# Macaron layer on one core: the minimum of the next unit moved ahead of P's low half on VectorE

## The chip, the cores and the metric

The kernel runs on one core of a Trainium2 chip. The metric is the device time in microseconds (us) of one execution, as the median of the runs.

## The reference

The input x is 4 x 256 tokens of width 512. Three residual steps follow one another:

```python
x = x + 0.5 * ffn(layernorm(x))      # dense 512x512 + bias + LoRA mixture, 8 experts of rank 16, top 2
x = x + attn(layernorm(x), wq, wk, wv, wo)
x = x + 0.5 * ffn(layernorm(x))
```

Attention has 32 query heads and 8 key/value heads of width 128, rotary embedding on q and k, a causal window of 128 keys, a softmax over each row, P times V, and the output projection `out @ wo`. All is float32. The kernel reaches that accuracy by splitting operands into a high and a low half (`_hi`, `_lo`) and adding three products.

## The kernel before

The middle part, some six sevenths of the time, is attention. It walks over eight **groups** g, one for each key/value head with its four query heads. Group 0 and group 7 are written out; groups 1 to 6 are a hardware loop on each engine. A group has two **halves** hf (two batches each), and a half has eight **slots** s, one for each **unit** u = 16g + 8hf + s: one batch with one query head. The order of work on each engine is written by hand, and every engine takes its own list in order; semaphores tie the lists together. Inside a slot of unit u:

- **TensorE (PE)**: at the first slot of a half (in the last half: at its third) the transposes of V (`v_transpose`, L1182), which wait for V's difference of the half before; a chunk of 9 matmuls of the projection that makes q, k and v of the next half (`project`, L1173; other counts in the first and last group); the scores of unit u+1 (`scores`, L1192 to L1195); the transposes of P of unit u-1 (`p_transpose`, L1203), which wait for the low half of P of unit u-2, since both use the one PSUM bank T; then, in slots 1 and 5, P times V (`values`, L1216), and in slots 2, 3, 6 and 7 the output projection (`out_project`, L1234).
- **VectorE (DVE)**: the softmax normalisation of unit u (`softmax_norm`, L918 and L921), which waits for the exponentials; where a projection ended in the slot before, the rotary sum (`rope_sum`, L888, both inputs in SBUF); where one ends now, the cosine product (`rope_cos`, L879); P's low half of unit u-1 (`p_lo`, L928), which waits for ScalarE's high half; in a slot where V's projection ends, V's difference (`v_diff`, L894); then the mask, fold and minimum of unit u+1 (`softmax_min`, L907 to L913), which waits for the scores of u+1; in slots 1 and 5 the low halves of the attention output (`o_lo`, L934); additions into x (`x_add`, L941) at slots 0, 3, 4 and 7.
- **ScalarE (ACT)**: exponentials of unit u (`softmax_exp`, L606), high halves of weights (L552), the rotary swap of a projection (`rope_swap`, L580), P's high half of unit u-1 (`p_hi`, L614), high halves of q and k (`rope_hi`, L588). In slots 1 and 5 `p_hi` also waits until `values` has read the old P.
- **GpSimd (POOL)**: the rotary sine product (`rope_sin`, L401), a masked copy of P (`p_part`, L408), which waits for `p_lo` of the same unit, the low half of q or k (`rope_lo`, L418), and the low halves of the weights (`split_lo`, L393): four of wo in slot 4 of a group's first half, which `out_project` needs in slot 6.

SP issues the weight loads, each when a slot of the ring of raw weights has been split.

V's projection ends in slot 7 of each half (in the last group in slot 1 of its second half), so `v_diff` runs there and `v_transpose` is the first work of TensorE in the next slot.

Of the kernel before, what the change touches and what calls it, by code (L numbers as in the profile page):

```python
# [46 lines left out]
SLOTS = 8  # L47
# [13 lines left out]
def ended(first, last, hf, s):  # L61

    if s < 0:
        return ended(first, last, 0, SLOTS - 1) if hf else None
    pos = spread(first, last, hf)
    return next((m for m in range(6) if pos[s] < 12 * (m + 1) <= pos[s + 1]), None)


def v_slot(last, hf):

    return 2 if last and hf else 0


def target(g, last, hf):

    return 2 * g + 1 if last else 2 * g + hf + 1
# [25 lines left out]
def macaron(nc, x_in, wq, wk, wv, wo, w_base, b_base, w_router, lora_a, lora_b, ident_in, mask_in, side_in, rope_in, out):  # L102
    ctx = ExitStack()
    with ctx:
# [126 lines left out]
        def wait(eng, s, n):  # L231

            if not isinstance(n, int) or n > 0:
                eng.wait_ge(s, n)
# [523 lines left out]
        def _(dve):  # L758
# [115 lines left out]
            def rope_cos(j, m):  # L874

                r = 5 * j + m
                dve.wait_ge(swap_done, r + 1)
                wait(dve, qlo_done, {0: r, 1: r - 2}.get(m, r - 1))
                nc.vector.tensor_tensor(rot[:, m % 2, :].rearrange("p (b s) -> p b s", b=2),  # L879
                                        A[m % 2][:, :].rearrange("p (b s) -> p b s", b=2),  # L880
                                        rope[:, 0 if m == 0 else 2, :].unsqueeze(1).broadcast_to([P, 2, SEQ]),
                                        ALU.mult).then_inc(a_free, 1)

            def rope_sum(j, m):
                r = 5 * j + m
                dve.wait_ge(t2_done, r + 1)
                dve.wait_ge(a_free, 6 * j + m + 1)
                nc.vector.tensor_tensor(rot[:, m % 2, :], rot[:, m % 2, :], swap[:, m % 2, :],  # L888
                                        ALU.add).then_inc(sum_done, 1)

            def v_diff(j):

                dve.wait_ge(vcopy_done, j + 1)
                nc.vector.tensor_tensor(v_half(swap[:, 1, :], 1), v_half(A[1][:, :], 1), v_half(swap[:, 1, :], 0),  # L894
                                        ALU.subtract).then_inc(vdiff_done, 1)

            def v_lo(j, par):
                dve.wait_ge(vhi_done, j + 1)
                nc.vector.tensor_tensor(v[1][:, par, :, :], A[1][:, :].rearrange("p (t n) -> p t n", t=HT),  # L899
                                        v[0][:, par, :, :].bitcast(F32), ALU.subtract).then_inc(a_free, 1)  # L900

            def softmax_min(u, s):

                dve.wait_ge(s_done, u + 1)
                wait(dve, exp_done, u - 1)
                sc = S[s % 2]
                nc.vector.tensor_tensor(sm[:, s % 2, 0:P], sc[:, P:2 * P], mask[:, 0:P], ALU.add).then_inc(part_done, 1)  # L907
                nc.vector.copy_predicated(sc[:, 2 * P:3 * P], mask[:, P:2 * P].bitcast(I32), sc[:, 3 * P:4 * P]).then_inc(part_done, 1)
                dve.wait_ge(part_done, 2 * u + 2)
                nc.vector.memset(gate[:, :], 0.0)  # L910
                nc.vector.tensor_tensor_reduce(sm[:, s % 2, 0:P], sc[:, 0:P], sm[:, s % 2, 0:P], 1.0, FMAX,
                                               ALU.add, ALU.min, nmax[:, s % 2, 0:1])
                nc.vector.tensor_reduce(nmax[:, s % 2, 1:2], sc[:, 2 * P:3 * P],  # L913
                                        axis=mybir.AxisListType.X, op=ALU.min).then_inc(min_done, 1)

            def softmax_norm(u, s):
                dve.wait_ge(exp_done, u + 1)
                nc.vector.reciprocal(rinv[:, s % 2, :], rsum[:, s % 2, :]).then_inc(rinv_done, 1)  # L918
                dve.wait_ge(rinv_done, u + 1)
                wait(dve, t_done, u - 1)  # L920
                nc.vector.tensor_tensor(prob[:, s % 2, 0:2 * P].rearrange("p (c n) -> p c n", c=2),  # L921
                                        S[s % 2][:, 0:2 * P].rearrange("p (c n) -> p c n", c=2),
                                        rinv[:, s % 2, :].unsqueeze(2).broadcast_to([P, 2, P]),
                                        ALU.mult).then_inc(norm_done, 1)

            def p_lo(u, s):
                dve.wait_ge(pthi_done, u + 1)
                nc.vector.tensor_tensor(pT[1][:, 0:2, s % G, :], T[:, 0:2 * P].rearrange("p (c n) -> p c n", c=2),  # L928
                                        pT[0][:, 0:2, s % G, :].bitcast(F32), ALU.subtract).then_inc(ptlo_done, 1)

            def o_lo(beta, par):
                for i in range(2):
                    dve.wait_ge(othi_done, 2 * beta + i + 1)
                    nc.vector.tensor_tensor(oT[1][:, par, i, :, :], O[i][:, :].rearrange("p (h n) -> p h n", h=G),  # L934
                                            oT[0][:, par, i, :, :].bitcast(F32), ALU.subtract).then_inc(otlo_done, 1)

            def x_add(beta, b, i):

                dve.wait_ge(c_done, 2 * beta + i + 1)
                wait(dve, x_added, 2 * beta + i)  # L940
                nc.vector.tensor_tensor(x[:, 2 * b + i, :], wo_bank(beta, i)[:, :], x[:, 2 * b + i, :], ALU.add).then_inc(x_added, 1)  # L941

            def ffn_start(s):

                if s in (0, 4):
                    norm_stats(2, s // 2)
                    norm_stats(2, s // 2 + 1)
                if s == 3:
                    x_lo(2, 0)
                    x_lo(2, 1)  # L950

            def group(g, first, last):
                for hf in range(2):
                    for s in range(SLOTS):
                        u, beta, b = 16 * g + 8 * hf + s, 4 * g + 2 * hf + s // G, 2 * hf + s // G
                        start = first and b == 0
                        split, m = (ended(first, last, hf, c) for c in (s - 1, s))
                        if s == v_slot(last, hf) and not (last and hf == 1):
                            v_lo(2 * g + hf, hf)
                        if s % G == 3 and not start:  # L960
                            x_add(beta - 1, (b - 1) % BATCH, 0)
                        if s % G == 0 and not (first and b < 2):
                            x_add(beta - 2, (b - 2) % BATCH, 1)
                        softmax_norm(u, s)
                        if split is not None and split < 5:
                            rope_sum(target(g, last, hf), split)
                        if m is not None and m < 5:
                            rope_cos(target(g, last, hf), m)
                        if not (start and s == 0):
                            p_lo(u - 1, s - 1)  # L970
                        if m == 5:
                            v_diff(target(g, last, hf))
                        if s == v_slot(last, hf) and last and hf == 1:
                            v_lo(2 * g + hf, hf)
                        if not (last and hf == 1 and s == SLOTS - 1):
                            softmax_min(u + 1, (s + 1) % SLOTS)
                        if s % G == 1 and not start:
                            o_lo(beta - 1, (b + 1) % 2)
                        if last and hf == 1:
                            ffn_start(s)  # L980
# [55 lines left out]
            rope_sum(0, 4)  # L1036
            softmax_min(0, 0)
            group(0, True, False)
            with dve.Fori(1, KV - 1) as g:
                group(g, False, False)  # L1040
            group(KV - 1, False, True)
            x_add(4 * KV - 2, BATCH - 2, 1)
            p_lo(16 * KV - 1, SLOTS - 1)
# [329 lines left out]
```

## Time and profile before

| what | value |
|---|---|
| median of 3 runs | 730.44 us (730.17 to 730.83) |
| the profiled execution | 729.86 us |
| its span in the profile | 728.1 us |
| TensorE busy | 712.6 us (98%) |
| VectorE busy | 521.3 us (72%) |
| ScalarE busy | 422.9 us (58%) |
| GpSimd busy | 403.8 us (55%) |
| granted TensorE clock | 1.00 |

Times in the trace count from the start of the span. "Busy" is the time in which the engine's instructions run; what an engine waits for is put down to the instruction whose semaphore came last.

### The profile page before, as it was taken

How to read it: one execution, taken by the hardware profiler on the slowest of the kernel's cores; microseconds unless marked ns; L12 is line 12 of the kernel's file. 1: busy time of each engine (PE TensorE's matmuls, PEld its weight loads, DVE VectorE, ACT ScalarE, POOL GpSimd, SP SyncE). 2: the span in 40 equal slices, each digit the busy share in tenths (PEclk: the TensorE clock that was granted, in tenths of full speed). 3: DMA queues.
4: the chain of work that ended last, by engine and by line, in shares of the span. 5: the costliest groups of instructions: out<-in, count | busy, mean ns of one | idle time of the engine just before them, and what ended most of it. 6: DMA issues, size and time to landing. Idle time of an engine off the chain costs nothing.

```text
span 728.1 us, 13744 instructions
## 1 busy us (share of the span) xinstructions
PE 712.6 (98%) x3692; PEld 601.4 (83%) x3692; DVE 521.3 (72%) x1773; ACT 422.9 (58%) x1144; POOL 403.8 (55%) x519
## 2 busy tenths in 40 slices
PE   8998989999999999999999999999999999999998
PEld 5786778888888888888888888888888888887886
DVE  6768676767776777677776677677767776778784
ACT  3455685657655676557655765476547665655440
POOL 2566677535863496437753765368535864374530
PEclk9999999999999999999999999999999999999999
DMA  8140003000310022002100120003000310030002
GB/s 277 43 174 30 0 20 112 14 1 2 102 45 1 0 72 72 1 1 72 58 15 1 58 72 15 1 22 96 26 2 0 98 32 0 1 117 1 1 30 87
DMA packets 25868, 32.33 MB, mean 44 GB/s; under 512 B 5833, under 2 KB 14281, under 8 KB 25298
## 3 DMA queue, kind: packets, MB, share of 16 engines
q1 hardware_dynamic: 25232, 30.69, 13.5%
q10 hardware_dynamic: 578, 1.05, 0.4%
q14 instruction: 44, 0.36, 0.2%
q8 instruction: 14, 0.23, 0.1%
HBM read 27.54 MB, written 4.19 MB: 44 GB/s over the span
## 4 chain that ended last, share of the span: by engine, by line
PE 87%; DVE 5%; POOL 4%; ACT 2%; issue 1%; DMA 1%; SPq 0%; DVEq 0%; POOLq 0%; ACTq 0%
PE bank L1173 33%; PE bank L1234 24%; PE bank L1216 8%; PE bank L1195 7%; PE bank L1137 4%; PE bank L1203 4%; PE bank L1192 2%; POOL wo_lo L393 1%; PE bank L1182 1%; PE bank L1193 1%; PE bank L1156 1%; DVE stats L775 1%; PE bank L1122 1%; DVE xnT_lo L798 1%; DMA x<-in_L_attn_x 1%
## 5 line engine op out<-in xcount | busy, mean ns | idle before, releaser
L401 POOL TENSOR_TENSOR swap<-swap,rope 128x512 f32<-128x512 f32 x80 | 104.8, 1310 | 112.5 <-ACT swap L580 112.2
L408 POOL TENSOR_SCALAR_AFFINE_SELECT pT_hi_lo<-pT_hi_lo 128x256 fp32r<-128x256 f32 x128 | 52.3, 409 | 143.5 <-DVE pT_hi_lo L928 143.5
L606 ACT ACTIVATE bank<-sm,nmax 128x128 f32<-128x128 f32 x128 | 47.6, 372 | 110.7 <-DVE nmax L913 110.5
L580 ACT ACTIVATE swap<-bank 64x512 f32<-64x512 f32 x160 | 95.0, 594 | 12.8 <-PE bank L1173 10.4
L614 ACT ACTIVATE pT_hi_lo<-bank 128x256 fp32r<-128x256 f32 x128 | 49.1, 384 | 91.4 <-PE bank L1203 63.0
L928 DVE TENSOR_TENSOR pT_hi_lo<-bank,pT_hi_lo 128x256 fp32r<-128x256 f32 x128 | 53.6, 419 | 50.4 <-ACT pT_hi_lo L614 50.1
L418 POOL TENSOR_TENSOR q_lo<-rot,q_hi 128x512 fp32r<-128x512 f32 x64 | 82.6, 1291 | 1.6 <-ACT q_hi L588 1.6
L1234 PE MATMUL bank<-wo_hi,oT_hi 128*128 128x512 f32 x256 | 74.6, 413 | 0.0
L1173 PE MATMUL bank<-xnT_lo,wq_hi 128*128 128x512 f32 x256 | 73.3, 390 | 0.0
L1173 PE MATMUL bank<-xnT_hi,wq_hi 128*128 128x512 f32 x256 | 71.9, 393 | 0.8 <-DVE v_lo L899 0.8
L1173 PE MATMUL bank<-xnT_hi,wq_lo 128*128 128x512 f32 x256 | 72.2, 394 | 0.0
L879 DVE TENSOR_TENSOR rot<-bank,rope 128x512 f32<-128x512 f32 x80 | 55.0, 687 | 23.7 <-ACT swap L580 23.6
L888 DVE TENSOR_TENSOR rot<-rot,swap 128x512 f32<-128x512 f32 x80 | 66.0, 825 | 6.5 <-POOL swap L401 6.3
L1234 PE MATMUL bank<-wo_lo,oT_hi 128*128 128x512 f32 x256 | 68.7, 390 | 1.6 <-POOL wo_lo L393 1.6
L1234 PE MATMUL bank<-wo_hi,oT_lo 128*128 128x512 f32 x256 | 68.6, 390 | 0.0
L1216 PE MATMUL bank<-pT_hi_lo,v_hi 128*128 128x512 f32 x192 | 62.1, 404 | 0.0
L1234 PEld LDWEIGHTS bank<-wo_lo,oT_hi 128*128 128x128 f32 x256 | 47.9, 188 | 12.7 <-POOL wo_lo L393 2.5
L921 DVE TENSOR_TENSOR prob<-bank,rinv 128x256 f32<-128x256 f32 x128 | 54.3, 424 | 4.9
L1195 PE MATMUL bank<-k_hi_lo,q_hi 128*128 128x256 f32 x256 | 57.7, 308 | 0.0
L1173 PEld LDWEIGHTS bank<-xnT_hi,wq_hi 128*128 128x128 f32 x256 | 47.5, 188 | 11.1 <-DVE v_lo L899 1.0
L1234 PEld LDWEIGHTS bank<-wo_hi,oT_lo 128*128 128x128 f32 x256 | 48.1, 188 | 10.1
L1173 PEld LDWEIGHTS bank<-xnT_lo,wq_hi 128*128 128x128 f32 x256 | 48.0, 188 | 10.1
(152 smaller groups left out, 1696.6 us busy)
## 6 DMA issues: line engine op xcount, KB each, us to landing
raw<-in_L_attn_wq SPq DMA_DIRECT2D x32, 256.0 KB, 3.0
raw<-in_L_attn_wo SPq DMA_DIRECT2D x32, 256.0 KB, 2.7
x<-in_L_attn_x SPq DMA_DIRECT2D x4, 512.0 KB, 7.4
raw<-in_L_attn_wk SPq DMA_DIRECT2D x8, 256.0 KB, 2.6
raw<-in_L_attn_wv SPq DMA_DIRECT2D x8, 256.0 KB, 3.4
out<-x SPq DMA_DIRECT2D x8, 256.0 KB, 2.0
raw<-in_L_ffn_W_base ACTq DMA_DIRECT2D x4, 256.0 KB, 5.2
wb_keep_hi<-q_hi SPq DMA_DIRECT2D x1, 1024.0 KB, 5.1
```

The costliest lines, as they stand in the source:

```text
L401: nc.gpsimd.tensor_tensor(w, w, tab, ALU.mult).then_inc(t2_done, 1)
L408: nc.gpsimd.affine_select(pT_both[:, :, 2, h, :], pT_both[:, :, 1, h, :].bitcast(F32), pattern=[[0, 2], [1, P]], compare_op=ALU.is_ge, fil ...
L418: nc.gpsimd.tensor_tensor(lo, rot[:, m % 2, :], hi.bitcast(F32), ALU.subtract).then_inc(qlo_done, 1)
L580: last = nc.scalar.activation(swap[a:a + half, m % 2, :], A[m % 2][b:b + half, :], ACT.Copy)
L879: nc.vector.tensor_tensor(rot[:, m % 2, :].rearrange("p (b s) -> p b s", b=2), A[m % 2][:, :].rearrange("p (b s) -> p b s", b=2), rope[:, ...
L888: nc.vector.tensor_tensor(rot[:, m % 2, :], rot[:, m % 2, :], swap[:, m % 2, :], ALU.add).then_inc(sum_done, 1)
L921: nc.vector.tensor_tensor(prob[:, s % 2, 0:2 * P].rearrange("p (c n) -> p c n", c=2), S[s % 2][:, 0:2 * P].rearrange("p (c n) -> p c n", c=2),
L928: nc.vector.tensor_tensor(pT[1][:, 0:2, s % G, :], T[:, 0:2 * P].rearrange("p (c n) -> p c n", c=2), pT[0][:, 0:2, s % G, :].bitcast(F32), ...
L1173: last = mm(A[m % 2][:, :], w, xnT[b][:, d, hf * HALF:(hf + 1) * HALF], start=(i == 0), stop=(i == 11))
L1195: last = mm(S[s % 2][:, 2 * P:4 * P], q[a][:, hf, h, q1], k[c][:, hf, b * SEQ:(b + 1) * SEQ], start=(n == 0), stop=(n == 2))
L1216: last = mm(O[i][:, :], v[a][:, par, 2 * b + kb, :], pT[c][:, blk, :, :], start=(n == 0), stop=(n == len(todo) - 1))
L1234: last = mm(wo_bank(beta, i)[:, :], oT[a][:, par, i, h, :], wo_s[c][:, h, :], start=(h == 0 and n == 0), stop=(h == G - 1 and n == 2))
```

## The change

In every slot of `group` on VectorE, `softmax_min(u + 1, ...)` is issued right behind the rotary work and in front of `p_lo(u - 1, ...)`, `v_diff` and, in the last half, `v_lo`. No instruction is added or taken away, and no semaphore changes. No other engine's list changes.

```diff
                             rope_sum(target(g, last, hf), split)
                         if m is not None and m < 5:
                             rope_cos(target(g, last, hf), m)
+                        if not (last and hf == 1 and s == SLOTS - 1):
+                            softmax_min(u + 1, (s + 1) % SLOTS)
                         if not (start and s == 0):
                             p_lo(u - 1, s - 1)
                         if m == 5:
                             v_diff(target(g, last, hf))
                         if s == v_slot(last, hf) and last and hf == 1:
                             v_lo(2 * g + hf, hf)
-                        if not (last and hf == 1 and s == SLOTS - 1):
-                            softmax_min(u + 1, (s + 1) % SLOTS)
                         if s % G == 1 and not start:
                             o_lo(beta - 1, (b + 1) % 2)
```

## Rows read from the trace of the kernel before

**Rows 1.** The page: share of the chain that ended last, by engine

```profile
PE 87%; DVE 5%; POOL 4%; ACT 2%; issue 1%; DMA 1%; SPq 0%; DVEq 0%; POOLq 0%; ACTq 0%
```

**Rows 2.** Windows, one half of a loop group: stretch, its length, busy us by engine

```profile
232.64:271.00 38.36, 38.36 (x199) 32.68 (x199) 27.40 (x92) 25.37 (x69) 22.33 (x23) 1.00 0.11 35
```

**Rows 3.** Timeline of TensorE, its stalls: start, us, instruction, idle before and releaser

```profile
99.78 0.41 PE L1203 MATMUL bank<-ident,prob 128*128 128x128 f32 x2 [0.80 <-DVE pT_hi_lo L928]
...
110.09 1.20 PE L1234 MATMUL bank<-wo_lo,oT_hi 128*128 128x512 f32 x4 [1.15 <-POOL wo_lo L393]
...
644.64 1.20 PE L1234 MATMUL bank<-wo_lo,oT_hi 128*128 128x512 f32 x4 [0.46 <-POOL wo_lo L393]
...
659.62 0.66 PE L1182 MATMUL bank<-ident,swap 128*128 128x128 f32 x4 [1.32 <-DVE swap L894]
```

**Rows 4.** Timeline of VectorE, one slot of the first group

```profile
93.30 0.17 DVE L918 RECIPROCAL rinv<-rsum 128x2 f32<-128x2 f32 x1 [0.91 <-ACT bank L606]
...
93.84 0.68 DVE L888 TENSOR_TENSOR rot<-rot,swap 128x512 f32<-128x512 f32 x1
...
95.13 0.41 DVE L928 TENSOR_TENSOR pT_hi_lo<-bank,pT_hi_lo 128x256 fp32r<-128x256 f32 x1
95.46 0.28 DVE L907 TENSOR_TENSOR sm<-bank,mask 128x128 f32<-128x128 f32 x1
...
96.20 0.29 DVE L913 TENSOR_REDUCE nmax<-bank 128x1 f32<-128x128 f32 x1
97.39 0.17 DVE L918 RECIPROCAL rinv<-rsum 128x2 f32<-128x2 f32 x1 [0.91 <-ACT bank L606]
```

**Rows 5.** Timeline of GpSimd in the first group

```profile
96.18 1.29 POOL L418 TENSOR_TENSOR q_lo<-rot,q_hi 128x512 fp32r<-128x512 f32 x1
...
103.39 0.41 POOL L408 TENSOR_SCALAR_AFFINE_SELECT pT_hi_lo<-pT_hi_lo 128x256 fp32r<-128x256 f32 x1 [1.84 <-DVE pT_hi_lo L928]
```

**Rows 6.** Timeline of all engines, first half of a loop group, slots 4 and 5

```profile
253.97 0.28 PE L1195 MATMUL bank<-k_hi_lo,q_lo 128*128 128x256 f32 x1
...
254.93 0.42 DVE L928 TENSOR_TENSOR pT_hi_lo<-bank,pT_hi_lo 128x256 fp32r<-128x256 f32 x1 [1.44 <-ACT pT_hi_lo L614]
...
259.85 0.42 DVE L928 TENSOR_TENSOR pT_hi_lo<-bank,pT_hi_lo 128x256 fp32r<-128x256 f32 x1 [0.71 <-ACT pT_hi_lo L614]
```

**Rows 7.** Timeline of all engines, slot 7 of that half and its end

```profile
267.09 1.29 POOL L418 TENSOR_TENSOR q_lo<-rot,q_hi 128x512 fp32r<-128x512 f32 x1
...
267.67 1.25 DVE L888 TENSOR_TENSOR rot<-rot,swap 128x512 f32<-128x512 f32 x1
...
268.85 0.41 DVE L928 TENSOR_TENSOR pT_hi_lo<-bank,pT_hi_lo 128x256 fp32r<-128x256 f32 x1
...
269.18 0.41 DVE L894 TENSOR_TENSOR swap<-bank,swap 128x256 f32<-128x256 f32 x1
...
270.39 0.60 PE L1182 MATMUL bank<-ident,swap 128*128 128x128 f32 x4
```

**Rows 8.** Timeline at the loop's return: last slot of a group, first of the next

```profile
228.95 0.28 PE L1195 MATMUL bank<-k_hi_lo,q_lo 128*128 128x256 f32 x1
...
231.32 0.29 DVE L913 TENSOR_REDUCE nmax<-bank 128x1 f32<-128x128 f32 x1
...
234.15 0.69 DVE L899 TENSOR_TENSOR v_lo<-bank,v_hi 128x512 fp32r<-128x512 f32 x1 [2.54 <-ACT v_hi L599]
...
236.57 0.17 DVE L918 RECIPROCAL rinv<-rsum 128x2 f32<-128x2 f32 x1 [1.14 <-issue]
...
237.21 0.41 DVE L928 TENSOR_TENSOR pT_hi_lo<-bank,pT_hi_lo 128x256 fp32r<-128x256 f32 x1
...
238.03 0.38 PE L1203 MATMUL bank<-ident,prob 128*128 128x128 f32 x2
```

**Rows 9.** Timeline of the last group, slot 4 of its first half

```profile
636.80 0.41 DVE L928 TENSOR_TENSOR pT_hi_lo<-bank,pT_hi_lo 128x256 fp32r<-128x256 f32 x1
...
637.48 0.42 POOL L408 TENSOR_SCALAR_AFFINE_SELECT pT_hi_lo<-pT_hi_lo 128x256 fp32r<-128x256 f32 x1
```

## The prediction, made before the changed kernel was run

> **What bounds the kernel now.** I read the page first: TensorE is busy 98% of the span (table above) and carries 87% of the chain that ended last [rows 1]. Then the windows: in a half of a loop group TensorE is busy all 38.36 us of 38.36, VectorE 27.40 [rows 2]. The 12 such halves (156 to 616 us) are alike. So nothing can be won there, and a delay is paid in full once it is longer than the cover of the wait that it feeds. Last I went through TensorE's timeline for its stalls. Those near a wait that the change touches are few [rows 3]: 0.80 for P's low half and 1.15 for the low halves of wo in the first group, 0.46 for the same of wo in the last group, 1.32 for V's difference near the end. All that the change could ever win lies in these and some smaller ones beside them.
>
> **What the change moves.** 126 minimum blocks pass P's low half (and 15 V's difference, one V's low half); nothing is added, no DMA is issued by VectorE. A minimum block takes from 95.46 to 96.20 + 0.29 = 96.49, so 1.03; neighbours overlap by some 0.08 (95.13 + 0.41 against 95.46), so it pushes what stands behind it back by about 0.94 [rows 4]. The exponentials, which wait for the minimum, come 0.33 earlier, the distance from 95.13 to 95.46. Behind P's low half wait two things: TensorE's transposes of the next unit and GpSimd's masked copy, with the low halves of q, k and the weights queued behind the copy on GpSimd. I go through the places by cover.
>
> *Slots 1 and 5.* P's low half waits 0.71 for its high half, which waits for P times V [rows 6]. The scores are long there, so the minimum fits in the wait: 0 to 0.15 later, 0.8 earlier for what follows. No gain, for TensorE does not wait.
>
> *Other slots of the loop.* The transposes start 1.4 us or more after the low half they need; only at the loop's return it is less. 0.94 is covered.
>
> *Slot 7 of a loop group's first half: the main term.* V's difference ends at 269.18 + 0.41 = 269.59 and TensorE takes it at 270.39: cover 0.80 [rows 7]. The change puts 0.94 ahead of it: 0.14 over. And VectorE comes to this slot late. In slot 4 the scores of the next unit are done at 253.97 + 0.28 = 254.25, so the minimum runs from about 254.29 and P's low half moves from 254.93 to 255.23, +0.30 [rows 6]. GpSimd's copy, q's low half and the four of wo follow without a gap, so the next sine product comes 0.30 later, the rotary sum and cosine behind it too, and GpSimd stays 0.30 late up to q's low half at 267.09, now 267.39. It matters because of the sum at 267.67: it takes 1.25 where others take 0.68 [rows 4, 7], and it ends at 268.92, 0.54 behind GpSimd's end at 268.38. In all 80 sums it is so: one that starts while GpSimd runs ends 0.54 behind GpSimd, one alone takes 0.68. So the sum ends at 267.39 + 1.29 + 0.54 = 269.22. Then the minimum from 269.15, P's low half 270.09, V's difference 270.42 to 270.83: TensorE starts at some 270.89 instead of 270.39, **+0.50, six times: +3.0**. Without the shift of GpSimd it is 0.2 x 6 = 1.2, my lower bound.
>
> *The same slot of the first group* has no sum and P's low half waits there; it costs 0. In the second halves V's difference has over 1 us of cover and comes at most 0.3 later: 0.
>
> *The first group: +1.65.* Its slots are not bound by TensorE: VectorE repeats in 97.39 - 93.30 = 4.09 [rows 4], a loop of normalisation, sum, cosine, P's low half, minimum and exponentials, against 3.54 of matmuls. The change takes 0.33 out of this loop. But P's low half is now last. In the slot before, one period ahead of 95.13, it moves from 91.04 to 91.98 and ends 92.39; GpSimd's copy starts 0.27 behind (as in [rows 9]), takes some 0.37, and k's low half runs 93.03 to 94.32 (1.29 [rows 5]). The normalisation starts at 92.96 instead of 93.30, the sum at 93.50 instead of 93.84: inside GpSimd's run. It ends 94.32 + 0.54 = 94.86, where before it ended 94.52; the cosine takes 0.61 to the next start, so the minimum starts 95.40 and P's low half 96.34 instead of 95.13. Before, GpSimd's low half ran in the gap behind the sum (96.18 to 97.47 [rows 5], between the sums at 93.84 and 97.39 + 0.54 = 97.93). The next slot alike: sum 97.87 to 99.22, P's low half 100.70 instead of 99.22. In the one after, which has no cosine, the sum runs 102.23 to 103.58, and P's low half ends 104.86; before it ended 0.2 ahead of the copy at 103.39, so at 103.20. GpSimd waits for just that (1.84 before 103.39 [rows 5]) and then does q's low half and the four of wo, for which TensorE waits at 110.09 [rows 3]. So this end moves by 1.65. Without collisions the sum is +0.2; that is the lower bound, 2.0 the upper.
>
> *The last group: +0.9.* In slot 4 P's low half starts right behind the cosine at 636.80, and GpSimd's copy 0.27 behind its end, at 637.48 [rows 9]; q's low half and the four of wo follow, and TensorE waits 0.46 for them [rows 3]. The scores are there, so the minimum's 0.94 goes through whole: the stall grows to 1.4. V's difference near the end follows P times V, with the minimum inside the wait: the 1.32 stays.
>
> *The loop's return: 0.* P's low half ends at 237.62 and TensorE takes it at 238.03, cover 0.41, of which some 0.15 go for the wake-up [rows 8]. +0.94 would stall 0.68 there, at five returns: 3.4 at most. But the first instruction of the new group starts 2.5 behind the end of the old one (231.61 to 234.15), and the normalisation loses another 1.14 to "issue": VectorE is late because it jumped late. Before the jump the scores are done at 228.95 + 0.28 = 229.23, and the minimum can now run in the wait for P's high half: minimum from 229.27, P's low half 230.21, V's difference 230.54 to 230.95, now the last instruction, 0.66 before 231.61. If the pause counts from there, P's low half moves by 0.94 - 0.66 = 0.28 against a cover of 0.26: a stall of 0.02. I take 0.1 in all.
>
> The Trainium skill, Runtime: NRT & Kernel Launch, "Instruction fetch mechanics", says that a taken branch out of the fetched pages stalls until the target has come by DMA; by that rule the pause hangs on VectorE's own jump, and the return costs nothing.
>
> The Trainium skill, SBUF — State Buffer, "Who interferes with whom", says that an elementwise instruction with two SBUF inputs and a GpSimd instruction reading SBUF exclude each other, and that who issued first goes on. The trace agrees by the 1.25 of the sum. By the rule the first group and slot 7 cost what I worked out, 4.65; if only durations of instructions run alone counted, 1.0 to 1.4.
>
> **Sum.** 3.0 + 1.65 + 0.9 + 0.1 = 5.65. The profiled execution took 729.86 for a span of 728.1; it would be 735.5. The median of the runs is 0.58 above it, so I predict **736.0**.
>
> **Rivals.**
> - *The delays are covered* (0.13): GpSimd catches up, the sums start before its low halves, V's difference stays within 0.2 of its cover. Left are 0.9 in the last group and less than 0.5 elsewhere: 731.0 to 731.9, no change. Against it: the cover of 0.80 is below 0.94 in six groups.
> - *A smaller cost* (0.18): slot 7 costs 0.14 to 0.3, the first group half: 732 to 734.
> - *The loop's return stalls as well* (0.15): if the pause does not move with VectorE, 0.4 to 0.7 x 5 more: 738 to 739.5.
> - *Faster* (0.04): the shorter loop of the first group, 3.76 instead of 4.09, wins back its stalls, 0.80 and those beside it and 1.15. The most is 2.9: 727.5. It decides by whether P's low half of the fourth unit ends before 103.20. For it speaks that the minimum does come earlier in each slot; against it, that GpSimd waits for P's low half and not for the minimum.
> - My forecast, 734 to 738: 0.50.
>
> A measurement of this kernel can tell about 0.2%, 1.46 us. Faster by more: 0.04; within: 0.14; slower: 0.82. The range 731.6 to 739.4 leaves out half of the first rival, the faster case, and the upper end of the third.
>
> **What the profile would show.** Right: TensorE idle before L1182, released by L894, some 0.5 six times, with V's difference behind the minimum; sums L888 of the first group at 1.3 instead of 0.68; the wait before L1234 near 645 at 1.4, and the first one near 111.7. No stall at L1203 behind the loop's return. The idle of VectorE in front of L928 falls from 50 us to a few. Wrong: if the sums slip in ahead of GpSimd's low halves, 4.65 shrinks towards 1.4; if TensorE stalls at L1203 in each loop group, the return counts.

## The result, and the profile after

The changed kernel takes **735.62 us** (median of 4 runs, 735.38 to 735.89), the kernel before 730.63 beside it (730.17 to 731.14): ratio 1.0071, 95% interval 1.0059 to 1.0083. It is slower, by 5.0 us; predicted were 736.0, in a range of 731.6 to 739.4. The profiled execution took 735.38, with a span of 733.7, at a granted clock of 0.998.

The page: share of the chain that ended last, and two groups of VectorE (busy, mean ns | idle before, releaser).

```profile
PE 72%; DVE 11%; POOL 8%; issue 6%; ACT 2%; DMA 1%; DVEq 0%; POOLq 0%; SPq 0%; ACTq 0%
L888 DVE TENSOR_TENSOR rot<-rot,swap 128x512 f32<-128x512 f32 x80 | 75.7, 946 | 10.2 <-POOL swap L401 10.0
L928 DVE TENSOR_TENSOR pT_hi_lo<-bank,pT_hi_lo 128x256 fp32r<-128x256 f32 x128 | 53.4, 417 | 14.0 <-ACT pT_hi_lo L614 13.8
```

The same two groups in the page of the kernel before:

```profile
L888 DVE TENSOR_TENSOR rot<-rot,swap 128x512 f32<-128x512 f32 x80 | 66.0, 825 | 6.5 <-POOL swap L401 6.3
L928 DVE TENSOR_TENSOR pT_hi_lo<-bank,pT_hi_lo 128x256 fp32r<-128x256 f32 x128 | 53.6, 419 | 50.4 <-ACT pT_hi_lo L614 50.1
```

TensorE's share of the chain fell from 87% [rows 1] to 72, VectorE's rose from 5 to 11, GpSimd's from 4 to 8 and that of "issue" from 1 to 6: the chain leaves TensorE more often. The 80 rotary sums (L888) take 946 ns on average, 825 before. The wait before P's low half (L928) was 50.4 us and is 14.0, since the minimum now fills it; the prediction had the direction right, but said "a few". That wait was no loss, so this large number tells nothing of the time.

Windows, all six loop groups: stretch, length, busy us of PE, PEld, DVE, ACT, POOL, clock, DMA share, GB/s.

```profile
156.00:616.00 460.00, 457.89 (x2359) 389.46 (x2358) 337.53 (x1095) 280.18 (x785) 270.68 (x275) 1.00 0.11 34
```

TensorE had no idle time in this stretch before (460.00 busy of 460.00, as in the half of [rows 2]) and has 460.00 - 457.89 = 2.1 now, six stalls of 0.35.

Timeline of TensorE: start, us, instruction, idle before and releaser. The stalls of the first group, the first of the six in the loop, and those of the last group.

```profile
101.11 0.41 PE L1203 MATMUL bank<-ident,prob 128*128 128x128 f32 x2 [1.88 <-DVE pT_hi_lo L928]
104.77 0.66 PE L1203 MATMUL bank<-ident,prob 128*128 128x128 f32 x2 [0.43 <-DVE pT_hi_lo L928]
111.50 1.20 PE L1234 MATMUL bank<-wo_lo,oT_hi 128*128 128x512 f32 x4 [0.68 <-POOL wo_lo L393]
...
272.89 0.66 PE L1182 MATMUL bank<-ident,swap 128*128 128x128 f32 x4 [0.35 <-DVE swap L894]
...
650.46 1.20 PE L1234 MATMUL bank<-wo_lo,oT_hi 128*128 128x512 f32 x4 [1.16 <-POOL wo_lo L393]
665.43 0.66 PE L1182 MATMUL bank<-ident,swap 128*128 128x128 f32 x4 [1.32 <-DVE swap L894]
```

Stalls alone don't add up to the loss. A surer reading sets the start of each matmul beside that of the same matmul before. The difference is 1.40 us behind the first group (the scores at 113.40 start at 114.80). It grows by 0.50 at each of the six L1182 (193.71 to 195.61, 270.39 [rows 7] to 272.89, and so on), with some 0.1 behind each, to 4.97 when the last group's slot 4 begins (the scores at 637.62 start at 642.59). The last group adds 0.84: 0.15 at the transposes of P in slot 4, which now wait for P's low half, and 0.69 before L1234 in slot 6 (5.12 to 5.81). At the start of the last dense layer the difference falls by 0.29 (5.83 to 5.54; the scores at 669.74 start at 675.28). It ends at 5.52; the spans differ by 5.6. A profiled execution can itself be late by some tenths before attention begins, where the code is the same: 0.04 here, up to 0.54 in the runs below.

Of the 0.50 at L1182 only 0.35 is shown as idle. Before, the transposes started 0.17 ahead of the recorded end of the matmuls in front (269.48 + 1.08 = 270.56, start at 270.39), with their weight loads begun at 270.17; now load and matmul both start at 272.89, and this overlap is lost as well. The transposes then take 0.66 instead of 0.60, which is part of the 0.1 behind each. Timeline of all engines around slot 7, as in [rows 7]:

```profile
269.10 0.17 DVE L918 RECIPROCAL rinv<-rsum 128x2 f32<-128x2 f32 x1
...
269.39 1.29 POOL L418 TENSOR_TENSOR q_lo<-rot,q_hi 128x512 fp32r<-128x512 f32 x1
...
269.64 1.59 DVE L888 TENSOR_TENSOR rot<-rot,swap 128x512 f32<-128x512 f32 x1
271.15 0.28 DVE L907 TENSOR_TENSOR sm<-bank,mask 128x128 f32<-128x128 f32 x1
272.09 0.42 DVE L928 TENSOR_TENSOR pT_hi_lo<-bank,pT_hi_lo 128x256 fp32r<-128x256 f32 x1
272.42 0.42 DVE L894 TENSOR_TENSOR swap<-bank,swap 128x256 f32<-128x256 f32 x1
...
272.89 0.42 PEld L1182 LDWEIGHTS bank<-ident,swap 128*128 128x128 f32 x4 [0.77 <-DVE swap L894]
```

The chain of the prediction is all there: GpSimd's low half ends at 270.68, the sum 0.55 behind it at 271.23, then the minimum, P's low half and V's difference, which ends at 272.84 with TensorE waiting.

### The profile page after: what moved, and what is told of

Its sections match the earlier page's. It is cut to its first block, busy times and chain, and to the rows that moved or that the text cites. A ratio compares the mean times of both kernels' runs of the same rounds, so it can differ in the third digit from the quotient of the medians.

```text
span 733.7 us, 13744 instructions
## 1 busy us (share of the span) xinstructions
PE 715.6 (98%) x3692; PEld 602.7 (82%) x3692; DVE 535.3 (73%) x1773; ACT 419.9 (57%) x1144; POOL 409.7 (56%) x519
## 4 chain that ended last, share of the span: by engine, by line
PE 72%; DVE 11%; POOL 8%; issue 6%; ACT 2%; DMA 1%; DVEq 0%; POOLq 0%; SPq 0%; ACTq 0%
PE bank L1173 27%; PE bank L1234 19%; PE bank L1216 7%; PE bank L1195 6%; PE bank L1137 4%; POOL wo_lo L393 4%; PE bank L1203 3%; DVE rot L888 2%; PE bank L1192 2%; POOL swap L401 1%; PE bank L1182 1%; DVE pT_hi_lo L928 1%; PE bank L1156 1%; DVE rot L879 1%; DVE stats L775 1%
## 5 line engine op out<-in xcount | busy, mean ns | idle before, releaser
L888 DVE TENSOR_TENSOR rot<-rot,swap 128x512 f32<-128x512 f32 x80 | 75.7, 946 | 10.2 <-POOL swap L401 10.0
L1234 PE MATMUL bank<-wo_hi,oT_hi 128*128 128x512 f32 x256 | 74.6, 413 | 0.0
L1234 PE MATMUL bank<-wo_lo,oT_hi 128*128 128x512 f32 x256 | 68.7, 390 | 1.8 <-POOL wo_lo L393 1.8
L1234 PE MATMUL bank<-wo_hi,oT_lo 128*128 128x512 f32 x256 | 68.5, 389 | 0.0
L928 DVE TENSOR_TENSOR pT_hi_lo<-bank,pT_hi_lo 128x256 fp32r<-128x256 f32 x128 | 53.4, 417 | 14.0 <-ACT pT_hi_lo L614 13.8
L1234 PEld LDWEIGHTS bank<-wo_lo,oT_hi 128*128 128x128 f32 x256 | 47.9, 188 | 12.9 <-POOL wo_lo L393 2.7
L1234 PEld LDWEIGHTS bank<-wo_hi,oT_lo 128*128 128x128 f32 x256 | 48.1, 188 | 10.1
```

The source lines that it names most:

```text
L1234: last = mm(wo_bank(beta, i)[:, :], oT[a][:, par, i, h, :], wo_s[c][:, h, :], start=(h == 0 and n == 0), stop=(h == G - 1 and n == 2))
```

## The experiments

All are compared with the kernel before, run again beside them on the same chip: it took 730.23 us beside runs 1 to 4, 730.12 beside runs 5 to 8 and 730.49 beside runs 9 and 10. The changed kernel's 735.62 was measured beside a 730.63, and it was not run again; so a difference between it and a run is uncertain by some 0.4 us, and for sizes below that the traces decide. Line numbers from the edit on count up to 5 more in some of them.

**1. The middles put back.** In slot 7 of each first half the old order on VectorE.

```diff
+                        late = hf == 0 and s == SLOTS - 1
-                        if not (last and hf == 1 and s == SLOTS - 1):
+                        if not late and not (last and hf == 1 and s == SLOTS - 1):
                             softmax_min(u + 1, (s + 1) % SLOTS)
                         ...                      # p_lo, v_diff, v_lo
+                        if late and not (last and hf == 1 and s == SLOTS - 1):
+                            softmax_min(u + 1, (s + 1) % SLOTS)
```

> The changed kernel, but in slot 7 of each group's first half the minimum stands behind V's difference again, as before. Theory (V's difference is the last thing that TensorE waits for at each mid-group boundary): the six stalls at L1182 are gone and with them the 0.55 that each group's first half grew by, 6 x 0.55 = 3.3 us; the time is 735.6 - 3.3 = 732.3 us, and the first group's 1.4 and the last group's 0.7 stay. Rival (the sums are slowed by GpSimd in all slots, and the loss is spread over the group): V's difference still ends late because the sum at this slot ends 0.3 later, and less than half of the 3.3 comes back, 734.0 us or more.

Measured: 731.88 (ratio 1.0020, interval 1.0011 to 1.0029). The stalls at L1182 are gone, and TensorE's delay does not grow in the loop groups: 1.41 us behind the first group, 1.31 before the last. So the middles cost 735.62 - 731.88 = 3.7 us, or 5.0 - 1.65 = 3.3 with each kernel set against the one before beside it (the trace has 3.6), and nothing else in the loop costs anything, the returns included. The sum at this slot still takes 1.59 here: slow sums alone did not delay TensorE.

**2. The first half of the first group put back.** The same edit with `late = first and hf == 0`.

> The changed kernel, but the first half of the first group keeps the order of before. Theory: its sums do not meet GpSimd's low halves, take 0.68 again instead of 1.26, and TensorE's wait for wo's low half ends at 110.1 instead of 111.5: 1.4 us less, 734.2 us. Rival (the stretch is bound elsewhere and what is lost here would be waited out later): no change, 735.6 us.

Measured: 734.60 (1.0063, 1.0049 to 1.0076). The first group's stalls are those of before (0.79, 0.67, 0.29, 1.15). The first group costs 735.62 - 734.60 = 1.0 by the medians, 5.0 - 4.4 = 0.6 with each set against its own before; the intervals of the two ratios overlap, so the medians alone don't size it. By the trace it is 1.4: the profiled execution of this kernel is already 0.5 late before attention begins, and no later behind the first group.

**3. The loop's return put back.** `late = hf == 1 and s == SLOTS - 1`: only in the last slot of a group is the minimum the last instruction of VectorE again.

> The changed kernel, but in slot 7 of each group's second half, the last before the loop returns, the minimum stands behind V's difference as before; slot 0 of the next group has the new order. Theory (VectorE's pause at the loop's return counts from its own last instruction): VectorE jumps some 0.6 us later, P's low half of slot 0 comes 0.6 later, and TensorE stalls 0.4 to 0.7 us at L1203 in slot 1 after each of five returns: 2 to 3.4 us more, 738.3 us. Rival (the pause ends at a time set by other engines): no stall, 735.6 us.

Measured: 740.28 (1.0135, 1.0120 to 1.0151): 4.7 us more than the whole change. Timeline of VectorE, ScalarE and TensorE at a return of this kernel:

```profile
233.70 0.29 DVE L913 TENSOR_REDUCE nmax<-bank 128x1 f32<-128x128 f32 x1
...
235.14 0.60 ACT L599 ACTIVATE v_hi<-bank 128x512 fp32r<-128x512 f32 x1 [0.28 <-PE bank L1185]
236.53 0.69 DVE L899 TENSOR_TENSOR v_lo<-bank,v_hi 128x512 fp32r<-128x512 f32 x1 [2.54 <-ACT v_hi L599]
...
238.81 0.17 DVE L918 RECIPROCAL rinv<-rsum 128x2 f32<-128x2 f32 x1 [1.00 <-issue]
...
240.39 0.41 DVE L928 TENSOR_TENSOR pT_hi_lo<-bank,pT_hi_lo 128x256 fp32r<-128x256 f32 x1
240.95 0.30 PE L1206 MATMUL bank<-ident,prob 128*128 128x128 f32 x1 [0.39 <-DVE pT_hi_lo L928]
```

and of the changed kernel:

```profile
232.57 0.42 DVE L894 TENSOR_TENSOR swap<-bank,swap 128x256 f32<-128x256 f32 x1
...
234.77 0.60 ACT L599 ACTIVATE v_hi<-bank 128x512 fp32r<-128x512 f32 x1 [1.57 <-PE bank L1182]
235.40 0.69 DVE L899 TENSOR_TENSOR v_lo<-bank,v_hi 128x512 fp32r<-128x512 f32 x1 [2.42 <-ACT v_hi L599]
...
237.39 0.17 DVE L918 RECIPROCAL rinv<-rsum 128x2 f32<-128x2 f32 x1 [0.69 <-issue]
...
238.96 0.41 DVE L928 TENSOR_TENSOR pT_hi_lo<-bank,pT_hi_lo 128x256 fp32r<-128x256 f32 x1
...
240.02 0.38 PE L1203 MATMUL bank<-ident,prob 128*128 128x128 f32 x2
```

The last instruction ends at 233.99 in one and at 232.99 in the other. Of this 1.00, 0.37 is that all of this execution is later here (L1182 at 234.42 and 234.05); the order accounts for 0.63. P's low half behind the jump is 1.43 later, 1.06 without the 0.37. ScalarE's high half of V (L599), for which L899 also waits, ends at 235.74 in run 3, and L899 starts only 0.79 later, 2.54 behind VectorE's last instruction. In the changed kernel it ends at 235.37 and L899 starts 0.03 behind it: there VectorE was already back, and V's high half sets the start. No other engine's order differs between the two, so what makes VectorE late at the return hangs on its own list, and the early minimum in the old group pays for the early minimum in the new one. The pause lies 2.45 to 2.63 behind the last instruction at all ten returns of run 3 and of the kernel before, and at most 2.4 behind it in the changed kernel. I had priced this at some 0.5 (738.3): TensorE loses some 0.9 at each return (stalls of 0.35 to 0.52, and another 0.43 to 0.47 in the overlap lost in front of the transposes, in the transposes and in P times V behind them).

**4. GpSimd's two instructions swapped in the changed kernel.** In each slot the low half of q or k goes ahead of the masked copy of P.

```diff
+                        if split is not None and split < 5:
+                            rope_lo(target(g, last, hf), split, 1 if last else 1 - hf)
                         if not (first and hf == 0 and s == 0):
                             p_part(16 * g + 8 * hf + s - 1, s - 1)
-                        if split is not None and split < 5:
-                            rope_lo(target(g, last, hf), split, 1 if last else 1 - hf)
```

> The changed kernel with GpSimd's order changed too: in each slot the low half of q or k goes ahead of the masked copy of P, so it does not wait for P's low half. Theory (the cost comes from GpSimd's low half being pushed into the rotary sum of the next slot, and from wo's low halves queued behind both): the first group's sums take 0.68 again and wo's low halves start 1.2 us earlier than in the kernel before, which takes away the stall of 1.15; V's difference is 0.2 us inside its cover; the last group's wait is that of before. Time 730.6 - 1.0 = 729.6 us, range 729.0 to 730.6. Rival (P's low half being 0.94 later costs by itself, collisions or not): the six stalls at L1182 stay at 0.2 to 0.5 each and the time is 732 us or more.

Measured: **728.91** (0.9979, 0.9970 to 0.9988), faster than both kernels, and a little below my range of 729.0 to 730.6. VectorE in the first group:

```profile
93.05 0.17 DVE L918 RECIPROCAL rinv<-rsum 128x2 f32<-128x2 f32 x1 [0.58 <-ACT bank L606]
...
93.59 0.68 DVE L888 TENSOR_TENSOR rot<-rot,swap 128x512 f32<-128x512 f32 x1
...
96.81 0.17 DVE L918 RECIPROCAL rinv<-rsum 128x2 f32<-128x2 f32 x1 [0.58 <-ACT bank L606]
```

Each sum takes 0.68 and the period is 3.76, against 4.09 before [rows 4]. There is no stall at L1182 in the loop groups; before L1234 there is 0.34 in the last group and still 0.29 in the first, where I had expected none.

**5. The minimum early in slots 1 and 5 alone.** `late = s % G != 1`.

> The minimum of the next unit stands early on VectorE only in slots 1 and 5 of each half, and late as before in the other six. My theory: what the early minimum costs comes from slots 7 (the group in the middle), from slots 1 to 3 of the first group and from slot 4 of the last; in slots 1 and 5 TensorE has cover for the one instruction more ahead of P's low half. So nearly all of the loss goes: 730.2 to 730.7 us, within 0.2% of before, with TensorE's stall before the output projection of the first group back near 1.15 us. Rival: the loss is spread over all slots (each late low half of P costs a little), and two slots in eight keep a quarter of the 5 us: about 731.9.

Measured: 730.17 (1.0001, 0.9992 to 1.0010), no change. Where the minimum fits into a wait, it costs nothing and wins nothing. The stall of 1.15 in the first group did not come back whole before the output projection, as I had expected: 0.72 of it stands before the transposes in front (108.68) and 0.23 before L1234, with TensorE some 0.1 to 0.2 later behind the group.

**6. The swap on GpSimd alone**, in the kernel before.

> The kernel before, with one change on GpSimd alone: in each slot the low part of the rotated result stands ahead of the masked copy of P. Theory: the run that has both (728.9) owes its gain over before to this swap, which lets VectorE's rotary sum run beside no work of GpSimd, and takes most of the 1.15 us stall before the first group's output projection; the order on VectorE then no longer matters, so this kernel comes out at 728.9 to 729.5 as well. Rival: the swap merely repairs the early minimum's harm, and the early minimum itself brings the gain; then this kernel stays at 730.2.

Measured: 730.26 (1.0002, 0.9993 to 1.0011). In the first group the sums take 0.68 and the period is 4.09, both as before. My theory fell: in the kernel before GpSimd is in nobody's way in the first group, so there is nothing to win by the swap.

**7. All three places put back at once.** `late` in slot 7 of the first halves, in the first half of the first group, and in slot 4 of the last group's first half.

> The changed kernel, with the old order in slot 7 of every first half, in the whole first half of the first group, and in slot 4 of the last group's first half. If the three losses are all there is and add up: 735.6 less 3.3 (the middles), less 1.4 (first group), less 0.7 (last group) = 730.2, and down to 729.9 if the quarter microsecond that came back at the last dense layer stays. Rival: the losses overlap or another stands behind them, and it stays above 731.

Measured: 729.68 (0.9995, 0.9986 to 1.0004). The losses add up, and what the trace shows as left is the 0.3 us that come back at the last dense layer. Runs 1 and 7 differ only in the first and the last group: 1.65 and -0.44 beside their own before, so the two cost 2.1 together, and 1.40 + 0.84 = 2.2 by the trace.

**8. GpSimd late, VectorE's order untouched**, in the kernel before:

```diff
+                        if first and hf == 0 and s in (1, 2, 3):
+                            for i in (2 * s - 2, 2 * s - 1):
+                                wait(pool, idled, i)
+                                nc.gpsimd.tensor_tensor(idle[:, :], rope[:, 0, :], rope[:, 1, :], ALU.mult).then_inc(idled, 1)
                         if not (first and hf == 0 and s == 0):
                             p_part(16 * g + 8 * hf + s - 1, s - 1)
```

> The kernel before, with VectorE's order untouched. GpSimd alone gets two additional multiplications of 128x256 (some 1.3 us together, their result unused) ahead of the masked copy of P, in slots 1 to 3 of the first half of the first group. That makes GpSimd's work lie beside VectorE's rotary sum, as the early minimum does, but VectorE's instructions stand where they stood. Theory (the sum that meets GpSimd's work is what costs in the first group): the sums in these slots take about 1.3 instead of 0.68 us and the group ends 1.2 to 1.9 us later, so 731.4 to 732.3. Rival (what costs there is only the minimum's own 0.9 us in front of P's low half, and GpSimd's delay is covered): 730.2 to 730.5 with sums near 0.7.

Measured: 732.35 (1.0029, 1.0018 to 1.0041). GpSimd and then VectorE in the first of these slots:

```profile
92.22 1.55 POOL L446 TENSOR_TENSOR idle<-rope 128x256 f32<-128x256 f32 x2
93.73 0.41 POOL L409 TENSOR_SCALAR_AFFINE_SELECT pT_hi_lo<-pT_hi_lo 128x256 fp32r<-128x256 f32 x1
94.11 1.29 POOL L419 TENSOR_TENSOR k_hi_lo<-rot,k_hi_lo 128x512 fp32r<-128x512 f32 x1
95.36 1.74 POOL L402 TENSOR_TENSOR swap<-swap,rope 128x512 f32<-128x512 f32 x1
```

```profile
94.33 1.61 DVE L893 TENSOR_TENSOR rot<-rot,swap 128x512 f32<-128x512 f32 x1
```

The low half ends at 95.40 and the sum at 95.94, 0.54 behind it. The slots repeat in 4.8 to 4.9 us. A rival would be that GpSimd's added 4.6 us themselves delay the low halves of wo. They don't: GpSimd has caught up by the fourth unit and waits for P's low half.

```profile
106.05 0.41 POOL L409 TENSOR_SCALAR_AFFINE_SELECT pT_hi_lo<-pT_hi_lo 128x256 fp32r<-128x256 f32 x1 [1.05 <-DVE pT_hi_lo L933]
```

The order on VectorE is the old one, so the collision alone makes the loss here. By the medians it is 2.2 us, just above my 1.2 to 1.9, with sums of 1.47 to 1.61 where the changed kernel has 1.26 to 1.28: the collisions are longer than those of the change, so the run shows the mechanism and not its size.

**9. The early minimum in the first group alone, with the swap.** `late = not (first and hf == 0)`, and GpSimd as in 4.

> The early minimum only in the first half of the first group, the old order on VectorE everywhere else, and the swap on GpSimd (low part of the rotated result ahead of the masked copy) in every slot. The swap alone gave nothing (730.26), so my theory that it brings the gain of the run with both fell. New theory: early, the minimum shortens a slot of the first group by 0.33 us (4.09 to 3.76), because the exponentials start that much sooner, and all that the swap does is keep GpSimd's work off the rotary sum. Then nearly the whole gain is here: a slot period of 3.76, TensorE 0.9 us earlier behind the first group, and a time of 730.2 less 0.9 = 729.2 to 729.4. Rival: the gain comes from the loop's groups, where the early minimum stands in 16 slots each; then this stays at 730.2.

Measured: 729.50, before 730.49 beside it (0.9989, 0.9980 to 0.9998). The period is 3.76 and TensorE is 0.93 early behind the first group. By the trace this is the whole gain of run 4 there (0.88, and 0.97 counted from the start of attention). The interval of the ratio just leaves out 1. Of the rest of run 4's gain 0.29 is the one at the last dense layer (-0.77 to -1.06), which run 9 lacks. Run 9 also loses 0.4 of its 0.93 again over the loop groups, in steps of 0.08 to 0.16 some 5 to 10 us behind four of the loop's returns; the cause of that was not tried.

**10. The swap in slot 4 alone**, in the changed kernel: GpSimd's low half of q ahead of its masked copy with `hf == 0 and s == 4`, and nowhere else.

> The changed kernel, with GpSimd's low part of the rotated result ahead of its masked copy of P in one slot alone, slot 4 of each first half. Theory: in the loop's middles the loss starts there. VectorE's late low half of P holds GpSimd's masked copy back, and behind it the rotated low part and the four low parts of the output weights (5.05 us), and those hold back the swapped product that VectorE's sum of slot 6 waits for. With the rotated low part done before, the weights start some 0.45 us sooner, and of the 0.55 us of each middle about 0.1 is left: 735.6 less 2.7 to 3.0 = 732.6 to 732.9, and down to 731.9 if the last group's 0.7 goes too. The first group's three slow sums (slots 1 to 3) stay. Rival: the middles' loss is made in slot 7 alone, by the minimum and its collision; then the stalls of 0.35 us stay and the time is 735.3 to 735.6.

Measured: 731.97 (1.0021, 1.0012 to 1.0030). GpSimd in slots 4 and 5 of a loop group:

```profile
256.41 1.30 POOL L418 TENSOR_TENSOR q_lo<-rot,q_hi 128x512 fp32r<-128x512 f32 x1 [2.33 <-ACT q_hi L591]
257.66 0.40 POOL L408 TENSOR_SCALAR_AFFINE_SELECT pT_hi_lo<-pT_hi_lo 128x256 fp32r<-128x256 f32 x1
258.03 5.05 POOL L393 TENSOR_TENSOR wo_lo<-raw,wo_hi 128x512 fp32r<-128x512 f32 x4
```

and in the changed kernel:

```profile
257.81 0.41 POOL L408 TENSOR_SCALAR_AFFINE_SELECT pT_hi_lo<-pT_hi_lo 128x256 fp32r<-128x256 f32 x1 [2.66 <-DVE pT_hi_lo L928]
258.19 1.29 POOL L418 TENSOR_TENSOR q_lo<-rot,q_hi 128x512 fp32r<-128x512 f32 x1
259.44 5.05 POOL L393 TENSOR_TENSOR wo_lo<-raw,wo_hi 128x512 fp32r<-128x512 f32 x4
```

The matmul stalls of 0.35 are gone. But TensorE's delay still grows from 0.74 behind the first group to 2.22 before the last: 1.48 in six groups, 0.25 each, against 0.60 in the changed kernel. So 0.35 of each middle came through GpSimd's queue and 0.25 is slot 7's own. The sum of slot 7 takes 1.59 here too, but it ends where it did before (268.23 + 1.59 = 269.82, less 0.91 of delay is 268.91, before 268.92), since GpSimd's low half is no longer late. I had expected 0.1 left per middle, which was too little, and had missed that slot 4 of the first group is swapped too, which gave 0.66 back there; the two errors cancel in the total. The last group's loss is gone as well.

## Why the prediction was right

The mechanism and the places held. The middles and the first group were put back alone, the loop's return was tested by run 3, and the last group only together with others (runs 7 and 10). In us of TensorE's delay:

| term | predicted | in the trace | runs |
|---|---|---|---|
| middles, 6 times | 3.0 | 3.6 | 3.3 to 3.7 (run 1) |
| first group | 1.65 | 1.40 | 0.6 to 1.0 (run 2) |
| last group | 0.9 | 0.84 | - |
| first and last together | 2.55 | 2.2 | 2.1 (runs 1 and 7) |
| loop's return | 0.1 | 0 | - |
| last dense layer | - | -0.29 | - |
| sum | 5.65 | 5.5 | 5.0 (medians) |

Part of the closeness is luck. The middles came out 0.6 dearer than the prediction had them, and the first group, the last group, the return and the unforeseen gain at the end together 0.7 cheaper.

*The middles.* The cover of 0.80 was overrun as worked out: 0.14 by the minimum alone, and 0.30 more because GpSimd was late since slot 4. Less TensorE's delay of 1.98 there, GpSimd's low half starts at 267.41 (predicted 267.39), the sum ends at 269.25 (269.22) and V's difference at 270.86 (270.83). Run 10 separates the two: 0.25 and 0.35 of the delay. My lower bound of 0.2 each was just this case without GpSimd's part. What I missed is that the matmuls behind a stall come later still: by some 0.05 right behind it and about as much again over the next two slots, both gone in run 1. That makes 0.60 out of 0.50; where the second half of it comes from was not traced.

*The first group.* The sums came as forecast: 1.28, 1.26 and 1.26 instead of 0.68, each ending 0.54 to 0.55 behind GpSimd's low half. The period became 4.26 and not 4.36, because GpSimd starts its copy 0.17 behind P's low half (96.70 to 96.87) and not 0.27. I had misread the row of the last group [rows 9]: GpSimd did not wait for P's low half there, it was still at its own sine product, as the timeline of the kernel before shows.

```profile
636.24 1.30 POOL L401 TENSOR_TENSOR swap<-swap,rope 128x512 f32<-128x512 f32 x1 [3.85 <-ACT swap L580]
```

That product ends at 637.54, and the copy at 637.48 stands right behind it. Where GpSimd does wait for P's low half, it starts 0.16 to 0.18 behind it, in all 65 such waits of the kernel before and all 110 of the changed kernel. P's low half of the fourth unit ends at 104.62, predicted 104.86, and the wo stall ends at 111.50, predicted 111.7. GpSimd and VectorE in the second of these slots, all engines in one timeline:

```profile
96.29 0.41 DVE L928 TENSOR_TENSOR pT_hi_lo<-bank,pT_hi_lo 128x256 fp32r<-128x256 f32 x1
...
96.87 0.41 POOL L408 TENSOR_SCALAR_AFFINE_SELECT pT_hi_lo<-pT_hi_lo 128x256 fp32r<-128x256 f32 x1 [0.88 <-DVE pT_hi_lo L928]
97.25 1.29 POOL L418 TENSOR_TENSOR q_lo<-rot,q_hi 128x512 fp32r<-128x512 f32 x1
...
97.83 1.26 DVE L888 TENSOR_TENSOR rot<-rot,swap 128x512 f32<-128x512 f32 x1
98.56 1.66 POOL L401 TENSOR_TENSOR swap<-swap,rope 128x512 f32<-128x512 f32 x1
```

Runs 8 and 9 show both sides of it. GpSimd late with VectorE untouched makes the loss; the minimum early with GpSimd out of the way makes a gain of 0.9. My rival "faster" had a real mechanism, the shorter loop of 3.76, and runs 4 and 9 have it. I gave it little because GpSimd waits for P's low half and not for the minimum, and that is what decided: only when GpSimd's low half no longer stands behind the masked copy is the loop free.

The Trainium skill, SBUF — State Buffer, "Who interferes with whom", was weighed in the prediction: by its rule 4.65 for the first group and slot 7, by durations of instructions run alone 1.0 to 1.4. The trace gave 1.40 + 3.57 = 5.0, and run 8 shows the exclusion with the order on VectorE unchanged. In one point the trace does not follow from the rule: the page calls the lock exclusive and, of VectorE's two-port modes, says that the loser fully blocks, but the GpSimd product that starts at 98.56 beside the sum (which ends at 99.09) is recorded as 1.66 instead of 1.29, so it loses 0.37 and not the whole 0.53. Whether its first 0.16 need no port or the two overlap, no run here shows.

*The last group.* The rows of the changed kernel, slot 4:

```profile
642.71 0.42 DVE L928 TENSOR_TENSOR pT_hi_lo<-bank,pT_hi_lo 128x256 fp32r<-128x256 f32 x1
...
643.30 0.41 POOL L408 TENSOR_SCALAR_AFFINE_SELECT pT_hi_lo<-pT_hi_lo 128x256 fp32r<-128x256 f32 x1 [0.78 <-DVE pT_hi_lo L928]
```

Less the 4.97 of TensorE's delay, P's low half starts at 637.74, 0.94 later than at 636.80, just as predicted. The copy starts at 638.33, 0.85 later than 637.48 and not 0.94, because it now waits for P's low half (0.17 behind its end), while before it stood behind GpSimd's own product. And the stall before L1234 went from 0.46 to 1.16, not 1.4, because TensorE pays 0.15 of the loss already in slot 4: before, P's low half ended at 637.21 and the transposes behind it started at 638.21, a cover of 1.00, which 0.94 and the time to wake use up. The prediction had overlooked this wait.

*The loop's return.* Right that it costs nothing, but not by a hair as I had it. P's low half ends 0.65 ahead of TensorE (239.37 to 240.02), where it was 0.41 [rows 8]; I had 0.13. The last instruction before the jump came as predicted (232.99 less 2.02 of delay is 230.97, predicted 230.95). The first behind it came 0.77 earlier (235.40 less 2.02 is 233.38, before 234.15) where I had 0.66, and was no longer set by the pause but by V's high half. And the wait for "issue" behind it shrank as well, from 1.14 to 0.69 (0.69 to 0.96 over the five returns, 1.03 to 1.14 before), which I had not foreseen. Why it shrank stays open. Had I believed the rival here, 0.4 to 0.7 each would have been too little: run 3 paid 0.9.

*Not foreseen:* 0.29 come back at 668 us. TensorE's first weight load of the last dense layer was idle 0.42 before, for "issue", and is not now. It shows in every run that keeps an early minimum in the last half (1 to 5, 7 and 10) and in none that doesn't (6, 8 and 9). That an input of that layer comes earlier on VectorE is only argued.

*The medians.* 735.62 - 730.63 = 5.0, the spans 5.6: the profiled execution of before was 0.58 under its first median, that of the changed kernel 0.24 under its own. My addition of 0.58 put the prediction some 0.4 above the measured median.

## What to carry to other kernels

Moving a block ahead of another on one in-order engine has to be followed into the queues that wait for the block which was passed. Here 0.35 x 6 + 1.40 + 0.69 = 4.2 of the 5.8 us of loss in the trace came by way of GpSimd, whose copy stood in front of work that had nothing to do with it. When an engine's order is changed, look for the order on its consumer that belongs to it: neither the early minimum (+5.0) nor the swap on GpSimd (0) gained anything alone, and together they gave -1.3. And a busy engine's delay is read from the starts of the same instruction in the two traces; the idle marked in front of the matmuls of the middles showed 2.1 of 3.6 us.

## What the runs showed of the hardware

A VectorE sum with both inputs in SBUF that starts inside a GpSimd instruction ends 0.54 to 0.56 us behind that instruction, whether it started 0.2 us into it (recorded as 1.61) or 0.6 (1.28). At a loop's return VectorE's first instruction comes 2.45 to 2.63 us behind its last in the kernel before and in run 3, with its input ready 0.7 to 0.9 before that start, and a few instructions later it waits 0.7 to 1.1 for "issue". GpSimd starts 0.16 to 0.18 us behind the VectorE instruction that it waits for. After a stall the two transposes of L1203 take 0.34 to the next matmul instead of 0.14 (240.95 to 241.29 in run 3, 240.02 to 240.16 in the changed kernel).
